# Who issues the stores of the expert phases: from SyncE's queue, mixed with the loads, to ScalarE's queue, behind its own copies

## What is computed

```python
h = einsum('bnd,hd->bnh', patchify(x, 16), W) + b          # 36 patches of 192 features
h = concatenate([cls_tok, h])                              # 37 tokens per image: 2368 rows of 192
h = h + attention(layernorm(h))                            # 12 heads of 16, a 3x3 neighbour term, softmax
x = layernorm(h)
w_fk = top4(softmax((x @ W_fk + b_fk) @ emb_fk_n.T))       # 4 of 128 experts, weights normalised
w_rk = top4(softmax((x @ W_rk + b_rk) @ emb_rk_n.T))
all_h = einsum('bsd,ndr->bsnr', x, f_know)                 # layer 0: 192 -> 128 for each expert
mid = einsum('bsnr,bsn->bsr', all_h, w_fk)
all_out = einsum('bsr,nrd->bsnd', mid, r_know)             # layer 1: 128 -> 192 for each expert
h = h + einsum('bsnd,bsn->bsd', all_out, w_rk)
```

## Time and profile before

| | us |
|---|---|
| runs, median (lowest to highest of 3) | 813.44 (807.11 to 814.75) |
| the profiled execution, its own time | 806.56 |
| its span, first to last instruction | 804.8 |
| TensorE matmuls busy | 546.0 (68%) |
| GpSimd busy | 403.8 (50%) |
| VectorE busy | 384.1 (48%) |
| ScalarE busy | 339.3 (42%) |
| SyncE's transfers, packet time as share of 16 DMA engines | 58.7% |
| GpSimd's transfers, the same | 11.6% |

### The profile page before, as it was taken

The page is one execution under the profiler, slowest core; times in us unless marked ns, Lnnn a source line. Parts: engine busy times, 40 slices in busy tenths (PEclk is TensorE's granted clock), DMA queues, the critical chain, the costliest instruction groups (busy, mean ns, idle before and its releaser), DMA issues.

```text
span 804.8 us, 16396 instructions
## 1 busy us (share of the span) xinstructions
PE 546.0 (68%) x5060; PEld 446.4 (55%) x5061; DVE 384.1 (48%) x1355; ACT 339.3 (42%) x738; POOL 403.8 (50%) x397
## 2 busy tenths in 40 slices
PE   6898998989898938506698859965007776687100
PEld 5686877868687826403477857765005455545100
DVE  2847678888797888999780001111101110032232
ACT  4246385664757435223355535542001554255100
POOL 2342360614324040676376007777766775466574
PEclk9689999999998978556599988996557999799655
DMA  5898679596860663296288747969958996599632
GB/s 137 289 350 340 224 288 369 195 409 210 334 264 22 137 125 79 85 282 170 84 254 268 200 132 214 269 190 335 288 165 239 279 288 202 170 296 285 184 96 71
DMA packets 151442, 177.44 MB, mean 220 GB/s; under 512 B 12777, under 2 KB 134930, under 8 KB 151378
## 3 DMA queue, kind: packets, MB, share of 16 engines
q1 hardware_dynamic: 138002, 149.20, 58.7%
q0 software_dynamic: 13376, 27.41, 11.6%
HBM read 76.55 MB, written 100.02 MB: 219 GB/s over the span
## 4 chain that ended last, share of the span: by engine, by line
PE 29%; DVE 20%; POOL 15%; issue 13%; DMA 10%; ACT 9%; SPq 3%; POOLq 0%; ACTq 0%; DVEq 0%
POOL gat L711 11%; PE bank L853 6%; DMA gat<-wide_dram,slots 5%; ACT qk_pad L1231 4%; PE bank L1141 4%; POOL mid_dram L719 4%; PE bank L900 3%; DVE pick L1840 3%; DMA xs<-mid_dram 3%; PE bank L1115 3%; PE bank L1130 3%; PE bank L838 2%; PE bank L1148 2%; DVE smax L1617 2%; DVE probs L1620 1%
## 5 line engine op out<-in xcount | busy, mean ns | idle before, releaser
L711 POOL DMA_INDIRECT gat<-wide_dram,slots x152 | 145.5, 957 | 110.0 <-SPq L547 54.4
L1390 ACT ACTIVATE os<-bank 128x256 f32<-128x256 f32 (+1 forms) x160 | 69.9, 437 | 135.7 <-PE bank L1141 63.0
L1115 PE MATMUL bank<-ident,xs 128*96 128x128 f32 (+1 forms) x480 | 89.1, 298 | 47.0 <-issue 19.1
L1887 DVE TENSOR_SCALAR acc<-gat,wts 128x128 f32<-128x128 f32 x19 | 5.8, 304 | 226.6 <-DMA gat<-wide_dram,slots 226.6
L1399 ACT ACTIVATE xsT<-bank 96x512 f32<-96x512 f32 (+1 forms) x160 | 76.1, 487 | 89.2 <-PE bank L1115 86.4
L655 POOL TENSOR_TENSOR qk_sum<-qk_pad 64x888 f32<-64x888 f32 x16 | 26.6, 1663 | 170.3 <-ACT qk_pad L1231 156.6
L698 POOL DMA_INDIRECT wide_dram<-x2b,slots x76 | 77.6, 1020 | 61.9 <-issue 57.2
L1141 PE MATMUL bank<-matrices,xsT 96*128 (+1 forms) x576 | 99.7, 313 | 2.1 <-ACT xsT L1399 1.8
L1115 PEld LDWEIGHTS bank<-ident,xs 128*96 128x96 f32 (+1 forms) x480 | 59.6, 164 | 72.8 <-issue 47.7
L719 POOL DMA_INDIRECT mid_dram<-comb,slots x76 | 74.1, 975 | 28.8 <-issue 22.4
L1141 PEld LDWEIGHTS bank<-matrices,xsT 96*128 96x128 f32 (+1 forms) x576 | 82.4, 203 | 8.6 <-issue 6.4
(11 more groups left out here) (187 smaller groups left out, 983.0 us busy)
## 6 DMA issues: line engine op xcount, KB each, us to landing
wide_dram<-zeros SPq DMA_DIRECT2D x6, 5632.0 KB, 19.5
mid_dram<-zeros SPq DMA_DIRECT2D x8, 2816.0 KB, 25.9
xs<-wide_dram SPq DMA_DIRECT2D x80, 192.0 KB, 3.4
wide_dram<-os SPq DMA_DIRECT2D x80, 192.0 KB, 3.6
matrices<-in_L_ffn_f_know SPq DMA_DIRECT2D x8, 1536.0 KB, 16.3
matrices<-in_L_ffn_r_know SPq DMA_DIRECT2D x8, 1536.0 KB, 12.6
wide_dram<-os SPq DMA_DIRECT2D x80, 128.0 KB
xs<-mid_dram SPq DMA_DIRECT2D x80, 128.0 KB, 3.8
```

Of the source, the lines that this page charges most:

```text
L711: pool.indirect_dma_start(gat[i][:, e, :], None, wide_dram[b], bass.IndirectOffsetOnAxis(ap=slots[:, t, k:k + 1], axis=0))\
L1115: last = pe.transpose(bank[r % 2][0:kp, c:c + ROWS], src, ident[:])
L1390: act.activation(os_[r][:, :, 0:width], bank[2 + r][:, 0:SB * width].rearrange("p (k w) -> p k w", w=width), ACT.Copy)\
```

## The change

SyncE keeps the loads and loses the stores. `next_rows` issues one load per unit; behind the loop it issues only the loads of the next phase, where there is one. In phase 1, where the matrices' loads behind it need all products to be over, a wait for all results' copies takes the place of the one that the last store held. `expert_end` is as before: SyncE still waits for the landing of all stores and adds to `experts_done`.

ScalarE issues the stores. In a step its order becomes X(0), X(1), R(0), X(2), S(0), R(1), X(3), S(1), R(2), S(2), R(3), S(3). Each store waits on `y_copied` for its own copy. S(0) and S(1) have another copy between theirs and themselves; S(2) and S(3) follow their copies directly. Bytes, transfers and semaphores' counts stay the same.

```diff
@@ SyncE, expert_rows
-                def store(s, r, copied):
-                    sp.wait_ge(y_copied[ph], copied)
-                    rows = wide_dram[b][bass.ds(s * (RING * SB * ROWS) + r * (SB * ROWS), SB * ROWS), 0:out_width]
-                    sp.dma_start(rows.rearrange("(k p) d -> p k d", p=ROWS), os_[r][:, :, 0:out_width])\
-                      .then_inc(y_stored[ph][r], 16)
-
-                def next_rows(s, first=False):
-
+                def next_rows(s):
                     for r in range(RING):
                         sp.wait_ge(t_filled[ph], s * RING + (r + 1))
                         load_rows(ph, s, r)
-                        if r > 0:
-                            store(s - 1, r - 1, s * RING + r)
-                        elif not first:
-                            store(s - 2, RING - 1, s * RING)
...
                 if ahead:
                     ahead()
-                for r in range(RING):
-                    if ahead:
+                    for r in range(RING):
                         sp.wait_ge(t_filled[ph], used * RING + (r + 1))
                         load_rows(ph + 1, 0, r)
-                    if r > 0:
-                        store(used - 1, r - 1, used * RING + r)
-                    else:
-                        store(used - 2, RING - 1, used * RING)
-                store(used - 1, RING - 1, used * RING + RING)
+                if ph == 1:
+                    sp.wait_ge(y_copied[ph], used * RING + RING)
@@ ScalarE, experts
+                def store(s, r):
+
+                    act.wait_ge(y_copied[ph], s * RING + (RING + r + 1))
+                    rows = wide_dram[b][bass.ds(s * (RING * SB * ROWS) + r * (SB * ROWS), SB * ROWS), 0:width]
+                    act.dma_start(rows.rearrange("(k p) d -> p k d", p=ROWS), os_[r][:, :, 0:width])\
+                       .then_inc(y_stored[ph][r], 16)
+
                 def step(s):
                     for r in range(RING):
                         act.wait_ge(t_filled[ph], s * RING + (RING + r + 1))
                         src = ...
                         act.activation(dst, src, ACT.Copy).then_inc(t_copied[ph], 1)
+                        if r > 1:
+                            store(s, r - 2)
                         if r > 0:
                             results(s, r - 1)
+                    store(s, RING - 2)
                     results(s, RING - 1)
+                    store(s, RING - 1)
```

More of the change, by code:

```diff
@@ L487, in expert_rows @@
                 layer, b = PHASES[ph]
-                out_width = (RANK, D)[layer]
                 used = sp.value_load(steps_used[0:1, b, layer:layer + 1], min_val=FIXED + 1, max_val=ALL_STEPS)
-                def store(s, r, copied):
-                    sp.wait_ge(y_copied[ph], copied)
-                    rows = wide_dram[b][bass.ds(s * (RING * SB * ROWS) + r * (SB * ROWS), SB * ROWS), 0:out_width]
-                    sp.dma_start(rows.rearrange("(k p) d -> p k d", p=ROWS), os_[r][:, :, 0:out_width])\
-                      .then_inc(y_stored[ph][r], 16)
-                def next_rows(s, first=False):
+                def next_rows(s):
                     for r in range(RING):
@@ L501, in next_rows @@
                         load_rows(ph, s, r)
-                        if r > 0:
-                            store(s - 1, r - 1, s * RING + r)
-                        elif not first:
-                            store(s - 2, RING - 1, s * RING)
                 for s in range(1, FIXED):
-                    next_rows(s, s == 1)
+                    next_rows(s)
                 if ph == 1:
```

## The result

The changed kernel takes **831.53 us** (median of 4 executions, 823.67 to 835.77). The kernel before, timed with it, took 814.10 (4 executions, 807.11 to 816.02). The ratio is 1.026, with a 95% interval of 1.021 to 1.032: slower by 17.4 us. (Medians are of all executions; ratios compare only the fast ones, those within 1.5% of the fastest of the same kernel.) The forecast was 811, with a range from 802 to 826; the time lies above the range.

What follows compares the result with a forecast made beforehand. It took engines to set phase 0's pace and late-issued loads to hold phases 2 and 3. Phase 0 +2.3, phase 2 -1.4 and the last gathers' earlier start -3.0 made -2.1 on 813.4: forecast 811 us, range 802 to 826.

Steps and rivals of the forecast that it cites:

- The ends: Ends of phases 0, 2, 3: last R no longer late, gathers start 3.1, 4.8 and 3.5 us sooner.
- The rival in which the ends don't come earlier: Ends of phases: SyncE's unused iterations, not the stores, hold `experts_done`; 817 us, chance 0.05.
- The price of one issue: Store on ScalarE's queue: issue takes 0.39 us as on SyncE, bounds nothing to 1.44.
- The slower rival: Step boundaries: issue dearer on ScalarE and visible at every boundary; +8.4 us, 822 us, chance 0.25.
- its +5.4 for phase 2: Phase 2 inside, upper bound: every store added and no wait shortened, +5.4 us.
- The boundary in phase 0: Phase 0, R(3) to X(0): S(3) adds 0.45 us per fixed step, 0.6 in the loop; +5.4 in all.
- Phase 2: Phase 2 inside: fixed part +0.4 us, loop steps 6.0 instead of 6.32 for -1.8; together -1.4.
- cover: Inside a step: S(0), S(1), S(2) issue while ScalarE would wait anyway; free in phase 0, S(0), S(1) perhaps 0.15 in phase 2.
- The floor itself: Phase 2's loop: DMA engines allow no step under 6.32 x 0.87 = 5.5 us.
- the faster rival: Phases 2 and 3: loads issued earlier, steps reach the DMA engines' limit; 803 us, chance 0.25.
- Phase 3: Phase 3 inside: boundaries cost 4.2 us against loads less late, +0.5 taken, bounds -2 and +4.2.
- The gathers suffer: GpSimd's first round in layer 1 takes 6 us longer than 65.2, its queue meeting two others; 816 us, chance 0.1.

Runs made afterwards that it cites:

- e4: Kernel before the change, with SyncE's last stores and the `experts_done` signal of phases 0, 2 and 3 put ahead of its unused iterations; 807.32 us, ratio 0.989.
- e1: Changed kernel without any stores of results or waits for their landing, so its output is not the reference's; 789.46 us, ratio 0.970.
- e2: e1 with each store's wait for its own copy put back, plus a semaphore addition, still nothing stored; 796.57 us, ratio 0.979.
- e5: Changed kernel with S(0) and S(1) back on SyncE, S(2) and S(3) still on ScalarE; 825.02 us, ratio 1.019.
- e7: Changed kernel unaltered, measured once more on another chip; 832.21 us, ratio 1.027.
- e3: Changed kernel with S(2) and S(3) moved behind X(0) and X(1) of the next step, all stores still on ScalarE; 804.79 us, ratio 0.989.
- e6: Changed kernel with S(2) and S(3) back on SyncE, S(0) and S(1) still on ScalarE; 809.07 us, ratio 0.996.
- e8: e3 measured once more on another chip; 803.92 us, ratio 0.988.

## Why the prediction was wrong

**The ends: right.** The last R's of phases 0, 2 and 3 are not late, and the gathers start 2.9, 5.4 and 4.3 sooner behind the last but one R, where the forecast had 3.1, 4.8 and 3.5. e4 shows the gains of phases 0 and 3 alone (4.2 and 3.6), not that of phase 2. The rival in which the ends don't come earlier falls.

**The price of one issue: right, and so half of its rival wrong.** 0.383 median on ScalarE against 0.390 on SyncE. The slower rival had the sign of the result and half of its size (+8.4, 822). Its first half, a dearer issue, is not what happened: it set 0.75 as the point where it decides, and 0.38 is what the issues at the boundaries take. Its second half, that every boundary shows its store, did happen, and more: even its +5.4 for phase 2, called every store added, is one store a step (4 x 0.45 + 6 x 0.6), where all four show. The Trainium skill (DMA: Bandwidth & Descriptors, Issuing engines are not separate DMA queues) says that a second issuing engine saves only the time of the issue, which is usually small beside the DMA. Both halves agree with this trace, 0.383 to issue and a median of 3.8 from issue to landing; but "small" is beside the transfer, and what counted was 0.38 beside the idle time of ScalarE's queue in a step, of which layer 1 had too little. By the Trainium skill (Perfetto Trace Analysis, DMA Instruction — HWDGE) a wait for the lock on the descriptor generator would have shown as a long issue; the longest of 160 was 0.932, so nothing here needs it.

**The boundary in phase 0: the size was off, and a part was missed.** Forecast 0.45 per fixed step and 0.6 in the loop; measured 7.58 - 6.95 = 0.63 (0.56 and 0.53 in the third and fourth fixed step) and 7.42 - 6.61 = 0.81. The sum took the store's address and its issue, 0.16 + 0.39, and "some for what follows", read off SyncE. It missed that ScalarE's queue runs ahead of its datapath: with the wait for R(3) the loop's register work can no longer run under R(3). e1 and e2 price that alone, 0.22 and 0.46. Cost: fixed +2.4 instead of 1.8, loop 6 x 0.81 = +4.9 instead of 3.6.

**The clock in phase 0: not foreseen.** Two steps of 9.06, 2 x 1.64 = +3.3. The granted clock was 1.00 in before's loop and fell in phase 0's loop only where TensorE stands idle for 1.6 together at every boundary of the loop (after, e5, e7). At most boundaries this is 1.25 in e2, 0.8 in before and e1, 0.83 to 0.87 in e3 and 0.63 in e6, and none of these has such a step there. But idle time alone doesn't explain it: in phase 2's loop of the changed kernel TensorE is idle for 0.97 and 1.47 at the boundary and the clock stays at 1.00, and the kernel before has its own drops in phases 2 and 3. That the change brought the two drops in phase 0 is shown by e7 and e5 having them as well; what makes the clock fall stays open. The three parts make phase 0's +10.5 (2.37 + 4.87 + 3.28 by unrounded steps).

**Phase 2: the wrong bound.** Forecast: fixed part +0.4, loop -1.8. Measured: 22.37 to 23.63, +1.3; loop 37.94 to 41.87, **+3.9**; and 0.6 more in the last step. Before's loop holds one step at the lower clock (7.39); its other five average 6.11, so that a step of 6.93 at full clock costs 0.8. With phase 3, which was worked out in the same way, this is the step that failed most. It held that late loads bind this phase and go on doing so, and that S(0), S(1) and S(2) have cover. With no stores a step takes 4.75 (e1), so there was more slack under the 6.32 than taken, 1.57; but ScalarE's queue had 2.2 to put in it, 0.55 for the waits and four issues with what belongs to them at 0.41 on average. Term by term (e1 to after): S(0) 0.34 and S(1) 0.23 instead of 0.15, S(2) 0.41 instead of nothing, S(3) with its wait 1.16 instead of 0.6. The floor itself wasn't far off: the 0.87 is of a stretch that runs 4.6 us past the loop, over the loop alone the share was 0.93, which makes it 5.9; e3 takes 5.76 (e8: 5.99) at a share of 0.98. The kernel after, at 0.84, doesn't come near it. SyncE's 22.6 us of waiting say that the loads had come off as the faster rival wanted, and it fell all the same, since ScalarE's queue was the next bound and not the transfers.

**Phase 3: the same, and the clock.** +8.1 inside instead of +0.5, and beyond its upper bound of +4.2: +2.2 in the fixed part and +5.9 in the loop. Four stores in series as in phase 2, and a clock of 0.83 in its loop, where the steps are 7.43, 7.68, 7.88 and 6.76 instead of 6.93: 2.0 of it. The step of 6.76 had a clock of 1.00, the other three 0.77 to 0.78, where before had one such step of four. How much of that is the clock and how much the loads (DMA share 0.88) I haven't separated. Phase 3 now sets the start of the last gathers alone, 8.0 later than GpSimd and VectorE were ready.

**The gathers suffer: wrong.** GpSimd's round took 66.1 instead of 65.2, where the rival needed 6 more, and it had 8.0 to spare.

**In all**: on the path the ends gave 7.2 us, where the forecast had 6.6, and the insides took 24.2, where it had 4.5. Where the order keeps the waits out of the boundary (e3), the same move of the stores is worth -8.5 us (e8: -9.6).

## What to carry to other kernels

Before moving a DMA issue to a compute engine's queue, count that queue and not the engine: its copies, issues and register work in a row, against the step. A store right behind the instruction that makes its data makes the queue wait for its own engine, which uncovers all the bookkeeping that follows; put it behind the next piece of independent work, as in e3, and most of the cost goes (a loop step of phase 0: 6.70, against 7.42, and 6.61 before). That work has to be long enough: in phase 0 the copy ahead of the store takes 0.59 and S(0) and S(1) cost nothing (e6), in phase 2 it takes 0.38 and they cost 0.34 and 0.23. A saving that is bound to an order at the end of a phase can often be had by itself (e4), and is a reason to try the order first.

## What the runs showed of the chip that I had not expected

- A queue's run-ahead is worth 0.22 us with no loop around and 0.46 to 0.55 with one: that is what a wait for the engine's own last instruction costs, with no DMA issued (e1 against e2).
- ScalarE's queue issues a DMA while the copy ahead of it runs, but not from its start. In e3 S(2) begins 0.26 behind the start of X(0) (449.05 to 449.31), although its data had been ready since before R(3). A store that still has to wait for its data starts 0.17 behind the end of their copy (S(1) and S(2) in phase 2). And the next copy comes 0.16 behind the issue's end (695.51 to 695.67), although its data had been there since 695.07.
- TensorE's granted clock fell to a mean of 0.81 over a whole loop step, with 48 products and transposes taking 7.47 instead of 5.83, in the three traces whose step boundaries in phase 0 hold 1.6 of idle time, and returned to 1.00 in the next step. In phase 2's loop of the same kernel, with 2.4 of idle time at the boundary, it stayed at 1.00. Before the fall TensorE had been busy 6.08 of 7.40; in e6, where it stayed at 1.00, 5.57 of 6.46.
